# Loads of the last stage's residual and normalised tokens in two blocks ahead of the experts, capacities in seven sizes, and no layer-norm statistics at the end

## The reference, cut to what is computed

```python
x = x + tanh(g_xattn) * attention(layernorm(x), ctx)     # 16 heads
h = layernorm(x)
logits = h @ gate_w.T                                    # 64 experts
topv, topi = top_k(logits, 8);  W = scatter(softmax(topv))
out = sum over e of ((silu(h @ gate_e.T) * (h @ up_e.T)) * W[:, e]) @ down_e.T
out = out + sigmoid(h @ sh_gate1.T) * shared_expert(h)
x = x + tanh(g_ffn) * out
```

## Time and profile before

| | us |
|---|---|
| median of 3 runs | 1716.02 (1713.53 to 1720.42) |
| the profiled execution, its own time | 1701.07 |
| its span, first to last instruction | 1699.2 |
| attention and routing, until the first list of an expert is loaded | 1139.4 |
| experts, to the last store that POOL issues | 456 |
| end, from there to the end of the span | 103 |

### The profile page before, as it was taken

How to read it: one execution, slowest core, us unless ns; L and a number is a source line. 1 busy time by engine, 2 the same in 40 slices (tenths; PEclk the granted TensorE clock), 3 DMA queues, 4 the chain that set the end, 5 groups by cost and what they waited for, 6 DMA issues and landing times. The chain is left out here.

```text
span 1699.2 us, 24951 instructions
## 1 busy us (share of the span) xinstructions
PE 1475.1 (87%) x7674; PEld 1194.8 (70%) x7674; DVE 1138.6 (67%) x2438; ACT 690.5 (41%) x1579; POOL 994.1 (59%) x1003
## 2 busy tenths in 40 slices
PE   7998999998999999999999897827799888888684
PEld 5766887776887776787777676616688887787552
DVE  5777780687882588783489747233567766677697
ACT  2333770111771111771011535203566665666431
POOL 3654670376773277673277753245666776767388
PEclk9999999999999999999999999957999999999798
DMA  7897205555104655103655042435678888888796
GB/s 246 296 317 274 71 6 161 183 169 150 37 6 125 193 171 171 41 6 112 190 170 149 23 153 74 149 93 183 203 252 265 288 287 269 283 271 272 304 367 271
DMA packets 157228, 308.04 MB, mean 181 GB/s; under 512 B 31390, under 2 KB 66808, under 8 KB 155256
## 3 DMA queue, kind: packets, MB, share of 16 engines
q1 hardware_dynamic: 131752, 241.76, 42.7%
q0 software_dynamic: 25344, 64.69, 12.2%
HBM read 236.72 MB, written 71.80 MB: 182 GB/s over the span
## 5 line engine op out<-in xcount | busy, mean ns | idle before, releaser
L1738 POOL TENSOR_TENSOR q_rope<-q_rope,q_sin 128x448 f32<-128x448 f32 x192 | 217.7, 1162 | 152.6 <-DVE q_sin L1110 152.4
L1744 POOL TENSOR_TENSOR prob<-prob,row_inv 128x375 f32<-128x375 f32 x209 | 168.4, 812 | 112.9 <-DVE row_inv L1132 110.5
L1819 POOL DMA_INDIRECT parts<-y_sb,t_rows x140 | 142.4, 1017 | 114.0 <-ACT y_sb L1635 82.9
L1812 POOL DMA_INDIRECT x_g<-xn_dram,t_rows x140 | 156.1, 1115 | 47.1 <-issue 42.4
L1759 POOL DMA_INDIRECT table<-entry,pos_i x128 | 126.3, 987 | 89.3 <-DVE count L1220 58.8
L797 PE MATMUL bank<-q_rope,m_w 128*128 128x448 f32 x384 | 159.6, 552 | 13.7 <-DVE q_tl L1116 9.0
L1110 DVE TENSOR_TENSOR q_sin<-bank,sin_q 128x448 f32<-128x448 f32 (+1 forms) x256 | 157.9, 617 | 4.0
L1124 DVE TENSOR_REDUCE row_max<-bank 128x1 f32<-128x375 f32 x224 | 119.3, 534 | 35.5 <-PE bank L699 35.0
L1635 ACT ACTIVATE y_sb<-bank,t_rows 112x512 f32<-112x512 f32 (+2 forms) x140 | 91.4, 689 | 103.9 <-PE bank L699 59.7
L1498 ACT ACTIVATE prob<-bank,row_max 128x375 f32<-128x375 f32 x224 | 128.3, 573 | 9.7 <-DVE row_max L1124 9.1
L823 PE MATMUL bank<-ident,prob 128*125 128x128 f32 x672 | 115.4, 282 | 19.0 <-POOL prob L1744 8.7
(11 more groups left out here) (297 smaller groups left out, 4619.9 us busy)
## 6 DMA issues: line engine op xcount, KB each, us to landing
w_gu<-in_w_gu SPq DMA_DIRECT2D x64, 512.0 KB
p_in<-parts SPq DMA_DIRECT2D x14, 2048.0 KB, 10.4
w_dp<-in_w_dp SPq DMA_DIRECT2D x64, 256.0 KB
m_w<-m_dram SPq DMA_DIRECT2D x48, 192.0 KB
wq_s0h<-wq_dram SPq DMA_DIRECT2D x24, 256.0 KB
wq_s0l<-wq_dram SPq DMA_DIRECT2D x24, 256.0 KB
wq_s1h<-wq_dram SPq DMA_DIRECT2D x24, 256.0 KB
wq_s1l<-wq_dram SPq DMA_DIRECT2D x24, 256.0 KB
```

The costliest lines, as they stand in the source:

```text
L1738: pool.tensor_tensor(o[:, c, :], o[:, c, :], q_sin[:, c, :], ALU.add).then_inc(s_radd, 1)
L1744: pool.tensor_tensor(prob[i][:], prob[i][:], row_inv[:, i:i + 1].to_broadcast([P, L]), ALU.mult)\
L1812: pool.indirect_dma_start(x_g[x % NXE][0:size, t, :], None, xn2_dram, bass.IndirectOffsetOnAxis(ap=t_rows[x % NROW][0:size, t, 0:1].bitcas ...
L1819: pool.indirect_dma_start(parts, bass.IndirectOffsetOnAxis(ap=t_rows[x % NROW][0:size, t, 1:2].bitcast(I32), axis=0), y_sb[x % NY][t][0:si ...
```

## The change

Four things are changed.

1. `KINDS` has seven capacities in place of three: 4 places of 288 rows (3 x 96), 8 of 276 (3 x 92), 8 of 256 (2 x 128), 12 of 240 (2 x 120), 16 of 224 (2 x 112), 8 of 208 (2 x 104) and 8 of 192 (2 x 96). Before there were 12 of 288, 20 of 256 and 32 of 224. The number of tiles is the same, 140; the rows of all places go from 15,744 to 15,072.
2. The residual and the normalised tokens are loaded as two blocks of 3.67 MB, `xs_all` and `base_all` (128x14x512), by SP behind the last stores of `END` and ahead of the weights of the first three experts. The 14 loads of `base_in` are gone. The loads wait for the output pass and for the landing of all stores of these tokens.
3. Statistics, scale, shift and `base_norm` are gone; `turn_base` reads `xs_all`.
4. `add_four` is `add_six`: DVE also adds two with two (128x1024), in place of POOL, which adds only one with one.

```diff
-KINDS = ((12, 96, 3), (20, 128, 2), (32, 112, 2))
+KINDS = ((4, 96, 3), (8, 92, 3), (8, 128, 2), (12, 120, 2), (16, 112, 2), (8, 104, 2), (8, 96, 2))
...
-        base_in = [kept(f"base_in{i}", [P, C]) for i in range(CT)]
+        base_all = kept("base_all", [P, CT, C])
+        base_in = [base_all[:, i, :] for i in range(CT)]
+        xs_all = kept("xs_all", [P, CT, C])
+        xs = [xs_all[:, i, :] for i in range(CT)]
...
             for step, b in END:
                 finish(step, b)
+            sp.wait_ge(s_o, len(PASSES) * H)
+            for i in range(2):
+                sp.wait_ge(s_xn2_st[i], 16 * B // 2)
+                sp.wait_ge(s_base_st[i], 16 * B // 2)
+            for dst, src in ((xs_all, xn2_dram[0:B * S, :]), (base_all, base)):
+                sp.dma_start(dst[:], src.rearrange("(i p) c -> p i c", p=P)).then_inc(s_base_in, 16)
             sp.wait_ge(s_order, 1)
...
-            for i in range(CT):
-                sp.dma_start(base_in[i][:], base[i * P:(i + 1) * P, :]).then_inc(s_base_in, 16)
...
-                    sp.wait_ge(s_p_pair, QC * NQ + 2 * (i - NC + 1))
+                    sp.wait_ge(s_p_pair, QC * NQ + i - NC + 1)
...
             def turn_base(i):
-                pe.wait_ge(s_nm2, B + i + 1)
+                if i == 0:
+                    pe.wait_ge(s_base_in, 32 + 32)
...
-            def add_four(i):
+            def add_six(i):
                 k = p_in[i % NC]
                 dve.wait_ge(s_p_in[i % NC], 16 * (i // NC + 1))
                 dve.tensor_tensor(k[:, 0:4, :], k[:, 0:4, :], k[:, 4:8, :], ALU.add).then_inc(s_p_add, 1)
+                dve.wait_ge(s_p_add, B + 2 * i + 1)
+                dve.tensor_tensor(k[:, 0:2, :], k[:, 0:2, :], k[:, 2:4, :], ALU.add).then_inc(s_p_add, 1)
...
-            for i in range(CT):
-                dve.bn_stats(base_stats[:, i, :], base_in[i][:]).then_inc(s_bn2, 1)
...
-            def base_norm(i):
...
-                pool.wait_ge(s_p_add, B + i + 1)
-                pool.tensor_tensor(k[:, 0:2, :], k[:, 0:2, :], k[:, 2:4, :], ALU.add).then_inc(s_p_pair, 1)
-                pool.wait_ge(s_p_pair, QC * NQ + 2 * i + 1)
...
+            for i in range(CT):
+                k = p_in[i % NC]
+                pool.wait_ge(s_p_add, B + 2 * (i + 1))
                 if i >= NC:
                     pool.wait_ge(s_p_out[i % NC], p_out_from + 16 * (i // NC))
+                pool.tensor_tensor(p_sum[i % NC][:], k[:, 0, :], k[:, 1, :], ALU.add).then_inc(s_p_pair, 1)
```

More of the change, by code:

```diff
@@ L345, in build @@
         p_sum = [kept(f"p_sum{i}", [P, C]) for i in range(NC)]
-        xs = [kept(f"xs{i}", [P, C]) for i in range(2)]
         xs_t = [kept(f"xs_t{i}", [P, CJ, P]) for i in range(2)]
@@ L1014, in turn_base @@
                 for j in range(CJ):
[L1015 removed]
+                    m = pe.transpose(bank[i % 2][:, j * P:(j + 1) * P], xs[i][:, j * P:(j + 1) * P], ident[:])
                 m.then_inc(s_x2tr, 1)
@@ L1416, in vector @@
             dve.wait_ge(s_pad, 6)
-            dve.wait_ge(s_base_in, 32 + 16 * CT)
-            for i in range(CT):
-                dve.bn_stats(base_stats[:, i, :], base_in[i][:]).then_inc(s_bn2, 1)
[L1420 to L1425, removed]
             for i in range(-AHEAD, CT + 1):
                 if 0 <= i < CT:
-                    add_four(i)
+                    add_six(i)
                 if i + AHEAD < CT:
@@ L1657, in scalar @@
             behind_loop(act, body)
-            def base_norm(i):
-                act.wait_ge(s_shift, B * RT + 1)
-                if i >= 2:
-                    act.wait_ge(s_x2tr, B + i - 1)
-                act.activation(xs[i % 2][:], base_in[i][:], ACT.Identity, bias=base_shift[:, i:i + 1],
-                               scale=base_scale[:, i:i + 1])\
-                   .then_inc(s_nm2, 1)
             def base_turn(i):
@@ L1844, in gpsimd @@
             behind_loop(pool, body)
-            def add_pairs(i):
-                k, o = p_in[i % NC], p_sum[i % NC]
-                pool.wait_ge(s_p_add, B + i + 1)
-                pool.tensor_tensor(k[:, 0:2, :], k[:, 0:2, :], k[:, 2:4, :], ALU.add).then_inc(s_p_pair, 1)
-                pool.wait_ge(s_p_pair, QC * NQ + 2 * i + 1)
+            for i in range(CT):
+                k = p_in[i % NC]
+                pool.wait_ge(s_p_add, B + 2 * (i + 1))
                 if i >= NC:
                     pool.wait_ge(s_p_out[i % NC], p_out_from + 16 * (i // NC))
-                pool.tensor_tensor(o[:], k[:, 0, :], k[:, 1, :], ALU.add).then_inc(s_p_pair, 1)
-            pool.wait_ge(s_bn2, 2 * B + 2 * CT)
-            pool.tensor_scalar(base_scale[:], base_mean[:, :, 1], EPS, None, ALU.add).then_inc(s_rs2, 1)
-            pool.wait_ge(s_rs2, 2 * B + 1)
-            pool.tensor_tensor(base_scale[:], base_scale[:], minus_half[:].to_broadcast([P, CT]), ALU.pow).then_inc(s_rs2, 1)
-            for i in range(CT):
-                add_pairs(i)
+                pool.tensor_tensor(p_sum[i % NC][:], k[:, 0, :], k[:, 1, :], ALU.add).then_inc(s_p_pair, 1)
         block = ctx.enter_context(nc.Block())
```

12 lines of the change are left out of this document (2 added, 10 removed).

## The result

On the chip of the table ahead, the changed kernel takes 1702.52 us (median of 6 runs, 1696.21 to 1703.13) and the kernel before 1713.72 (6 runs, 1710.75 to 1720.42): a ratio of 0.9935, with a 95% interval of 0.9912 to 0.9958. Forecast were 1700.7 us in a range of 1691 to 1710, a ratio of 0.9911 to the median shown then. The number held; three of its terms did not, and on another chip the sign turned round. There the kernel before takes 1626.30 us and the changed one 1647.89, a ratio of 1.0139 (1.0112 to 1.0165).

A forecast was written before the change was run, and what follows sets the result against it. PE was taken to pace the experts, DVE and POOL taking turns, with transfers near the same limit, the end. Terms -4.5, +2 and -12.7 sum to -15.2 us: 1685.9, scaled to 1700.7 us, range 1691 to 1710.

The forecast's parts named there:

- Start of the end: First `p_in` tiles: without statistics, DVE adds tile 0 at its landing; the last landing comes 7.5 us earlier.
- additions moved: Last stage: DVE's second addition worth 0.1 us a tile; steps behind the last landing 10.5 us, not 15.7 (-5.2).
- Rival A: Last stage: DVE keeps waiting for POOL, 5.9 us a tile; end gains only 5.6 us, scaled 1707.9; chance 0.18.
- Blocks in the gap: Between attention and experts: two block loads delay weights and first list, +2 us.
- rival B: Gap before the experts: blocks load at 319 GB/s and hold up the experts, +7.2 us, scaled 1706.0; chance 0.13.
- Step 3: Between experts and last stage: removing the `base_in` loads gives 0, allowing up to -2 us.
- Rival C: Gap before the experts: blocks load at 194 GB/s, +26.8 us, scaled 1725.7, slower overall; chance 0.03.
- Capacities: Experts, paced by PE: fewer columns and smaller transposes save 4.5 us, with bounds of 6.9 us and nothing.
- no gain in the experts: Experts: the new row counts save nothing, scaled 1705.2; chance 0.04.
- The tail: Behind the last sum: 4.8 us for the last store, as before, so no change.
- a constant 0.9%: Whole kernel: profiled execution lies 0.9% under the median of runs, so 1685.9 us was scaled to 1700.7.
- Rival D: Experts: one token over a place's capacity starts the serial loop of 64 bodies, over 770 us; chance 0.02.

The follow-up runs named there:

- the third set: Last four follow-up kernels, on variants of the changed kernel's capacities and block loads, run beside the kernel before (1625.97 us, 27 runs): 1620.13, 1622.66, 1624.77 and 1663.15 us.
- the ladder: Changed kernel with 12 places of 3 x 96 rows, 8 of 2 x 128, and four each of row counts from 126 down to 100: 1663.15 us.

## Why the prediction was right, and where it was not

**Start of the end, additions moved: right.** Landing, order and pace are as worked out: 5.5 us a tile from the transfers, 5.6 us from the last landing at 1687.46 to the end of the last sum at 1693.08 (5.7 forecast). The stage gained 10.9 us and not 12.7: the first landing comes 8.5 us behind its issue and not 7.7, and the transfers lose 1 us more on the way. The 5.2 us behind the last landing came as forecast (from there to the end of the last sum 10.9 us before, 5.6 after). The 0.1 us a tile for the moved addition did not show: in mid-stage it is worth nothing, and behind the last landing 3.5 us, which the sum had in its 5.2.

**Rival A (DVE paces the end): refuted** for the changed kernel by L1395 at 0.15 us and DVE waiting 0.7 us a tile, and its mechanism shown in the kernel with POOL's addition back, where the 1.22 us return. Its condition was that POOL is working when L1395 comes.

**Blocks in the gap: right in kind, mis-sized, and in part a wash.** The list is late by 2.1 us in the first trace, as summed, but I stopped at the list: the first tanh is late by 4.2 (4.6 on the third set's chip), within the 7.2 of rival B. Step 3, the missing `base_in` at 0, was right: from the last tanh to the first `p_in` it is 9.8 us with these loads and 9.8 without, in the kernel with the old capacities. But both blocks at that place would cost 2.9 us there and 7 x 0.34 in the last places, some 5 us, so the gap is no dearer a place for them than the other. Rival C (slower, below 236 GB/s; its own terms give 240) did not come: blocks and weights move at 287 to 401 GB/s between 1116 and 1142.

**Capacities: wrong, and this is the step that failed.** It read "the lower is nothing, if POOL's indirect DMAs, whose number stays, or the transfers pace them". The number stays, but not the price of one. I had no row with 92, 104 or 120 rows and took the price of 96, 112 and 128 for all, so the bound should have gone below nothing. On a quick chip, where POOL paces the experts, the term is +24.5 us in place of -4.5. On the slow one the traces give +4.5, as POOL had waits to spend: 14.9 us more of work there, 10.3 less of idling. Which places lose there isn't plain from one trace of each, since those of 92 rows take 7.7 us, under the 8.1 forecast. The rival to which I gave 0.04, no gain in the experts, was the nearest, and even it stopped at nothing. And the -4.5 was worked out from PE's columns, which don't set the pace on the quick chips: with multiples of 16 and fewer columns at the last eight places the time stays that of the old capacities.

**The tail: a term read wrongly.** "And then, as before from 1694.4 to 1699.2, 4.8 us for the store" is 8.1 us, and it is POOL's drain in both kernels; the store lands 2.0 us behind its issue. But for the ladder the drain is 6.62 us long in each kernel without 92 rows, and 9.89 in each one with them. It isn't simply the sum of small packets: in the ladder, with three times as many of 8 bytes, it is 5.97. What it waits for stays open.

**Why the total was right all the same.** By its stages my sum said -15.2 us against the trace, and the trace says +2.0. The medians say -11.2, since the profiled execution of before lies 9.7 us under the quickest of its timed runs, and the changed one at its median. I had scaled that lag away as a constant 0.9%. It isn't one: other profiled executions lie from 6 us under the median of their kernel to 8 us above it. Of the -11.2 us, -10.9, +3.3 and +4.2 stand in the traces of stages that hardly vary; the rest, some -8 us, must lie in the experts or the attention of the ordinary executions of before, which no trace shows. Why the same change gives 0.9935 on that chip and 1.0139 on another is thus explained in part, by POOL's slack; that part makes it lose less there, and doesn't show a gain. That 1700.7 and 1702.52 lie so close is luck: a capacity term with the wrong sign and a tail at nothing were made up for by a lag that no trace explains.

**Slips in the working** that move nothing: the worst case of the range adds up to 1717.6 and not 1716, and the six tiles to 1661.5 end with the tenth landing, not with "the ninth one after" the fourth.

**Rival D (a capacity overflows)** did not come; 140 gathers in each trace leave no serial loop.

## What to carry to other kernels

Before a row count of an indirect DMA is changed, take its largest divisor up to 16 and count the rows of one share: 96 rows are cheaper than 92 for the engine that issues them, and a pad row can be worth more than it costs. An engine whose busy time plus a constant gap fills the window paces the stage, whatever its busy share on the page says; POOL stood at 61% of the span on the quick chip and was the limit of a fifth of it. And measure a change by its parts and on more than one chip: here a gain of 0.4% and a loss of 1.6% had been folded into one, and the chip decided which was seen.

## What the hardware showed that was not expected

- GpSimd's time for one indirect DMA is 0.92 us for 96 rows, 1.18 for 92, 1.67 for 122; above nine rows of a share it goes by them, 0.013 us each.
- Shares that carry no data still get packets, of 8 bytes for each pair and 4 for a single row: 6,912 packets of 8 bytes in the changed kernel, none before.
- The last drain of GpSimd ends the span; it takes 6.62 us (5.97 in the ladder), and 9.89 with 92-row transfers in the kernel, 350 us and more after the last of them.
- Two chips differ by 66 us in the expert stage of one kernel (420.7 and 354.8 us), with the same spacing of matmuls, and by 10 us in the gap ahead of it (56.8 and 46.8), but not in all that comes before (1111.4 on the slow one, 1106.9 to 1115.0 in the traces of the others). What makes the one slow there stays open; its DMA moved 262 GB/s and the other's 316.
